# Between the mixtures: the residual as an identity product, row sums and centred squares on ScalarE

## The reference, cut to what matters

```python
def _layernorm(x, axis=-1, eps=1e-05):
    m = jnp.mean(x, axis=axis, keepdims=True)
    v = jnp.var(x, axis=axis, keepdims=True)
    return (x - m) / jnp.sqrt(v + eps)
...
    def _L1_xattn_ref(hidden_states, memory_tokens, memory_mask):
...
        scores = jnp.einsum('bsd,bmd->bsm', hidden_states, memory_tokens) * scale
...
        attn = jax.nn.softmax(scores, axis=-1)
        readout = jnp.einsum('bsm,bmd->bsd', attn, memory_tokens)
...
    x = x + _L1_xattn_ref(_layernorm(x, axis=-1), ctx_2048, mask_BxS2_bk0)
    x = x + _L1_ffn_ref(_layernorm(x, axis=-1), L1_ffn_router_w, L1_ffn_w_gate, L1_ffn_w_up, L1_ffn_w_down)
```

## Time and profile before

| | us |
|---|---|
| median of three timed executions | 1752.46 |
| lowest, highest | 1746.93, 1753.07 |
| the profiled execution | 1746.06 |
| its span, first to last instruction | 1744.3 |
| mean granted TensorE clock (1 is 2.4 GHz, 0.50 is 1.2 GHz) | 0.929 |
| the stage `middle`, SyncE's first load to VectorE's last list | 848.5 to 1001.2 |

### The profile page before, as it was taken

How to read it: one execution, slowest core, us unless ns; L and a number is a source line. 1 busy time by engine, 2 the same in 40 slices (tenths; PEclk the granted TensorE clock), 3 DMA queues, 4 the chain that set the end, 5 groups by cost and what they waited for, 6 DMA issues and landing times. The chain is left out here.

```text
span 1744.3 us, 34265 instructions
## 1 busy us (share of the span) xinstructions
PE 1519.5 (87%) x8762; PEld 1174.2 (67%) x8763; DVE 1364.7 (78%) x2831; ACT 1060.6 (61%) x2044; POOL 777.8 (45%) x515
## 2 busy tenths in 40 slices
PE   4578899998888989999589569999999999999990
PEld 3546666666566867777347348888887778878880
DVE  6835867867787458888377869999999999999992
ACT  1124645635454468887134158888888888888870
POOL 5010000110301325554101248887887878788870
PEclk9588999999999999999775679999999999999995
DMA  9215537354560367755735129888888888998778
GB/s 338 98 44 131 117 74 213 79 119 125 119 184 1 98 228 173 159 107 91 207 116 192 64 73 215 173 174 186 189 186 185 167 209 196 236 215 164 132 121 308
DMA packets 170175, 270.58 MB, mean 155 GB/s; under 512 B 20080, under 2 KB 95856, under 8 KB 167856
## 3 DMA queue, kind: packets, MB, share of 16 engines
q0 software_dynamic: 46448, 108.85, 32.5%
q1 hardware_dynamic: 123632, 160.57, 31.2%
HBM read 151.62 MB, written 91.16 MB: 139 GB/s over the span
## 5 line engine op out<-in xcount | busy, mean ns | idle before, releaser
L1969 DVE TENSOR_TENSOR moe_w_lo<-moe_w_up,moe_w_hi 128x1536 fp32r<-128x1536 f32 (+1 forms) x180 | 325.9, 1811 | 1.7 <-ACT moe_w_hi L1793 1.7
L1744 POOL DMA_INDIRECT moe_rows<-moe_rows,moe_ids x200 | 282.4, 1412 | 66.7 <-issue 58.8
L1793 ACT ACTIVATE moe_w_hi<-moe_w_up 128x1536 fp32r (+2 forms) x180 | 273.7, 1520 | 0.0
L2082 PE MATMUL psum<-moe_w_hi,moe_rows_hi 128*128 128x384 f32 (+1 forms) x720 | 262.8, 365 | 3.6 <-DVE moe_rows_lo L1963 3.6
L2083 PE MATMUL psum<-moe_w_lo,moe_rows_hi 128*128 128x384 f32 (+1 forms) x720 | 248.7, 345 | 0.0
L2084 PE MATMUL psum<-moe_w_hi,moe_rows_lo 128*128 128x384 f32 (+1 forms) x720 | 248.7, 345 | 0.0
L1755 POOL DMA_INDIRECT moe_sum<-moe_res,moe_ids x100 | 189.6, 1896 | 96.4 <-ACT moe_res L1831 48.4
L1755 POOL DMA_INDIRECT moe_other<-moe_res,moe_ids x100 | 187.6, 1876 | 87.6 <-ACT moe_res L1831 38.2
L2092 PE MATMUL psum<-moe_w_down,moe_hid_t 128*128 (+1 forms) x400 | 205.0, 594 | 0.0
L862 ACT ACTIVATE prob<-psum,neg_top 128x128 f32<-128x128 f32 (+3 forms) x256 | 133.1, 528 | 80.2 <-DVE neg_top L1052 74.9
L1963 DVE TENSOR_TENSOR moe_rows_lo<-psum,moe_rows_hi 128x512 fp32r<-128x512 f32 x200 | 138.3, 691 | 19.5 <-ACT moe_rows_hi L1776 12.6
(11 more groups left out here) (356 smaller groups left out, 3367.1 us busy)
## 6 DMA issues: line engine op xcount, KB each, us to landing
q_st<-unit SPq DMA_DIRECT2D x128, 128.0 KB, 3.0
k_st<-unit SPq DMA_DIRECT2D x128, 128.0 KB, 3.1
moe_w_up<-in_L_ffn_w_gate SPq DMA_DIRECT2D x32, 384.0 KB, 5.2
moe_w_up<-in_L_ffn_w_up SPq DMA_DIRECT2D x32, 384.0 KB, 6.1
moe_w_down<-in_L_ffn_w_down SPq DMA_DIRECT2D x32, 256.0 KB, 6.5
moe_w_down<-in_L_ffn_w_down SPq DMA_DIRECT2D x64, 128.0 KB, 7.0
moe_sum<-x_sb SPq DMA_DIRECT2D x4, 1024.0 KB, 4.4
moe_sum<-m_x_sb SPq DMA_DIRECT2D x4, 1024.0 KB, 4.7
```

The lines of the kernel that those rows point to most:

```text
L1744: pool.indirect_dma_start(rows[u][:, :], None, d["rows"], bass.IndirectOffsetOnAxis(ids[:, t:t + 1], 0)).then_inc(gathered[u], 16)
L1793: sc.activation(w_hi[u % SPLITS][:, :], up_of(at), ACT.Copy).then_inc(T["wh"], 1)
L1969: v.tensor_tensor(w_lo[u % SPLITS][:, :], up_of(at), w_hi[u % SPLITS][:, :].bitcast(F32), ALU.subtract).then_inc(T["wl"], 1)
L2082: mm(ps[:, 2 + i, 0:2 * I], hi, w_h, start=(k == 0), stop=False)
```

## The change

It does four things between the mixtures.

1. The residual: after each attention product a second product, of the identity with the tile of x, adds x into the same PSUM bank. VectorE's `residual` is gone; ScalarE copies the bank into x and sums the rows on the way.
2. Statistics: ScalarE makes minus the mean from the row sum, then squares each tile with that as bias and sums the squares. VectorE makes the variance from them (`variances`, `second_variances`). This holds for the second norm of all batches and for the first norm of batches 1 to 3. The row sum of those comes from the addition of the tables. The squares themselves are written to places that are overwritten later.
3. The two filler products between logits and `attended` are gone.
4. Orders: the context is loaded after two pairs of tables; GpSimd's norm of batch 3, VectorE's softmax of batch 0 and sums of batch 3, and ScalarE's rows stand elsewhere.

The core of the diff:

```diff
@@ sync
-            sp.dma_start(ctx_sb[:, :, :], a["ctx_2048"].rearrange("b k d -> k b d")).then_inc(S["ctx"], 16)
             tables(0, 2, x_in[0])
             tables(2, 2, x_in[1])
+            sp.dma_start(ctx_sb[:, :, :], a["ctx_2048"].rearrange("b k d -> k b d")).then_inc(S["ctx"], 16)
...
@@ gpsimd
-            first_norm(3)
             for b in range(BATCH - 1):
                 second_norm(b + 1)
+                if b + 3 < BATCH:
+                    first_norm(b + 3)
                 write_runs(pool, m, b, run_ids[b][:, :], r1["slots"], S["slotted"])
...
@@ scalar
+            def squares(u, b, spare):
+
+                act.wait_ge(S[f"minus{u + 1}"], b + u)
+                for t in range(TPB):
+                    n = tile(b, t)
+                    sc.activation(spare(b, t), x[:, n, :], ACT.Square, bias=minus[u][:, n:n + 1],
+                                  accum_out=square[u][:, n:n + 1]).then_inc(S[f"square{u + 1}"], 1)
+
+            def minus_mean(u, b):
+                of_batch = slice(tile(b, 0), tile(b + 1, 0))
+                sc.activation(minus[u][:, of_batch], total[u][:, of_batch], ACT.Copy, scale=-1.0 / D).then_inc(S[f"minus{u + 1}"], 1)
+
+            def statistics(b):
+                act.wait_ge(S["added"], b)
+                minus_mean(0, b)
+                squares(0, b, lambda b, t: xn[:, t, :])
+
+            def residual(b):
+                for t in range(TPB):
+                    n = tile(b, t)
+                    act.wait_ge(S["o"], n + 1)
+                    sc.activation(x[:, n, :], ps[:, 6 + t % 2, :], ACT.Copy, accum_out=total[1][:, n:n + 1]).then_inc(S["x3"], 1)
+                act.wait_ge(S["x3"], tile(b + 1, 0))
+                minus_mean(1, b)
+                squares(1, b, lambda b, t: hn[:, tile(b, t), :])
...
@@ vector
+                        own.did(v.scalar_tensor_tensor(x[:, n, :], x[:, n, :], 1.0, x_other[:, n, :], ALU.mult, ALU.add,
+                                                       accum_out=total[0][:, n:n + 1]))
...
+            def variances(b):
                 of_batch = slice(tile(b, 0), tile(b + 1, 0))
+                dve.wait_ge(S["square1"], TPB * b)
+                v.tensor_scalar(var[:, of_batch], square[0][:, of_batch], 1.0 / D, EPS, ALU.mult, ALU.add).then_inc(S["var"], 1)
...
-                    v.tensor_tensor(at, at, ps[:, 6 + t % 2, :], ALU.add).then_inc(S["x3"], 1)
...
+            def second_variances(b):
+                dve.wait_ge(S["square2"], TPB * (b + 1))
+                v.tensor_scalar(var2[:, :], square[1][:, tile(b, 0):tile(b + 1, 0)], 1.0 / D, EPS, ALU.mult, ALU.add).then_inc(S["var2"], 1)
...
             add_tables(1)
-            statistics(1)
+            softmax(0)
+            variances(1)
+            shares(0)
             shift_of(1)
-            softmax(0)
-            shares(0)
             add_tables(2)
-            residual(0)
+            second_variances(0)
...
@@ tensor
-                    mm(ps[:, 6 + t % 2, :], att_t[:, t, :], ctx_sb[:, b, :], start=True, stop=True).then_inc(S["o"], 1)
+                    o = ps[:, 6 + t % 2, :]
+                    mm(o, att_t[:, t, :], ctx_sb[:, b, :], start=True, stop=False)
+                    mm(o, ident, x[:, tile(b, t), :], start=False, stop=True).then_inc(S["o"], 1)
...
                 if b + 1 < BATCH:
-                    keep_busy(nc, m, c, 2, 5, True)
                     attended(b + 1)
```

More of the change, by code:

```diff
@@ L2196, in middle @@
         shift, shift2 = sb("shift", [P, TILES]), sb("shift2", [P, TPB])
+        total, minus, square = [[sb(f"{n}{u}", [P, TILES]) for u in range(2)] for n in ("sum_of", "minus", "square")]
         r = {n: sb("r_" + n, [P, TPB, size]) for n, size in (("prob", N), ("logit", N), ("value", 8), ("total", 1), ("mask", N))}
@@ L2310, in _ @@
             normed_out(0)
-            normed(1)
+            statistics(1)
             exponents(0)
             attention_out(0)
+            normed(1)
+            residual(0)
             for b in range(BATCH):
@@ L2317, in _ @@
                     normed_out(b + 1)
+                if b + 2 < BATCH:
+                    statistics(b + 2)
                 hidden(b)
@@ L2327, in _ @@
                     normed(b + 2)
+                if ahead:
+                    residual(b + 1)
         @block.vector
@@ L2362, in shift_of @@
                 dve.wait_ge(S["rstd"], b + 1)
[L2363 removed]
+                v.tensor_tensor(shift[:, of_batch], minus[0][:, of_batch], rstd[:, of_batch], ALU.mult).then_inc(S["shift1"], 1)
             def shift_of_hidden(b):
                 dve.wait_ge(S["rstd2"], b + 1)
[L2367 removed]
+                v.tensor_tensor(shift2[:, :], minus[1][:, tile(b, 0):tile(b + 1, 0)], rstd2[:, :], ALU.mult).then_inc(S["shift2"], 1)
             def softmax(b):
@@ L2384, in shares @@
                 v.tensor_tensor(att[:, :, :], att[:, :, :], den[:, :].unsqueeze(2).to_broadcast([P, TPB, KEYS]), ALU.mult).then_inc(S["p"], 1)
-            def residual(b):
-                for t in range(TPB):
-                    dve.wait_ge(S["o"], tile(b, t) + 1)
-                    at = x[:, tile(b, t), :]
-                    v.tensor_tensor(at, at, ps[:, 6 + t % 2, :], ALU.add).then_inc(S["x3"], 1)
-                    dve.wait_ge(S["x3"], tile(b, t) + 1)
-                    own.did(v.bn_stats(stats2[:, t, :], at))
-                own.wait()
-                for t in range(TPB):
-                    own.did(v.bn_aggr(mv2[:, t, :], stats2[:, t, :]))
-                own.wait()
-                v.tensor_scalar(var2[:, :], mv2[:, :, 1], EPS, None, ALU.add).then_inc(S["var2"], 1)
+            def second_variances(b):
+                dve.wait_ge(S["square2"], TPB * (b + 1))
+                v.tensor_scalar(var2[:, :], square[1][:, tile(b, 0):tile(b + 1, 0)], 1.0 / D, EPS, ALU.mult, ALU.add).then_inc(S["var2"], 1)
             def shift_logits(b):
@@ L2454, in _ @@
             add_tables(0)
-            statistics(0)
+            statistics()
             normed(0)
@@ L2494, in _ @@
                 if ahead:
-                    residual(b + 1)
+                    second_variances(b + 1)
             run_starts(BATCH - 1)
```

33 lines of the change are left out of this document (16 added, 17 removed).

## The result

| | us |
|---|---|
| after, median of four executions | 1796.3 (1783.12 to 1803.01) |
| before, measured beside it, four executions | 1752.76 (1746.93 to 1753.77) |
| ratio | 1.023, 95% interval 1.018 to 1.0281 |
| profiled execution of after | 1783.12, span 1781.3, mean clock 0.913 |

The change makes the kernel 2.3% slower, 43.5 us by the medians. The forecast, 1782, had the direction; the time lies 5 us above the upper end of its range, 1791.

The account below looks back on a forecast made before the run. TensorE at half clock was taken to bound the long stretch, a chain between engines the short ones. Batches +35.8, start -3.5 and end +3.1 gave +35.4 us on 1746.06, 1781.5, taken as 1782; range 1756 to 1791.

Parts of the forecast that it names:

- Direction and mechanism: Stage between the mixtures: ScalarE's copy and squares make TensorE pause, the clock falls after batch 0 and stays down; +35.4 us.
- eight products: Attention plus identity products of one batch on TensorE: 14.25 us at half clock, 7.3 at full.
- third flip: Next batch's third tile flip, waiting for ScalarE to empty a bank: starts 4.55 us after the last product, bounds 4.3 and 5.0.
- logits stage: Part of a batch between scores and transposes: 10.2 us at half clock.
- transposes and copy: Small transposes and their copy ahead of a batch's eight products: 1.75 us at half clock.
- Sum of three: Three batches at half clock, 39.4 us each: 118.2 us where before are 82.4, so +35.8.
- Start: Stage start up to batch 0's last product: reordered loads and earlier softmax end it sooner, -3.5 us.
- End: After the last batch's products: 6.9 us to the first normed flip instead of 4.9, logits at half clock; +3.1 us.
- B: Rival: identity products bring the clock back within each eight; +23.4 us, 1769 us; chance 0.22.
- D: Mixed rival: the clock falls in only one or two of three batches, 12 us each above C; 1756 to 1768; chance 0.13.
- C: Rival: full clock throughout, pairs carrying it over the waits; batch 27.4 us, -2.2 us, 1744 us; chance 0.1.
- Row sums: VectorE's table sums gain a row sum: between nothing and 0.2 us more each, taken as 0.1.

Follow-up runs that it names:

- e8: The changed kernel without identity products: VectorE adds out of PSUM with a row sum, ScalarE still squares the new rows; stage 163.4 us, ratio 1.0212.
- e3: The changed kernel with the residual's part undone, so VectorE adds and takes those statistics again; stage 145.9 us, ratio 0.9914 from five of ten executions.
- e7: The kernel before with only the identity products added, VectorE copying where it added, fillers kept; stage 172.6 us, ratio 1.0199.
- e2: The changed kernel with ScalarE emptying the next batch's four flips before squaring the residual's tiles; stage 189.0 us, ratio 1.0264.
- e13: The changed kernel with four filler products in each of two pauses per batch, behind the second flip and behind the scores; stage 172.5 us, ratio 1.0181.
- e11: The changed kernel with attention products widened from 64 to 128 partitions by zeros; stage 170.5 us, ratio 1.0177.
- second executions: The kernel before and the changed kernel, both unchanged, each profiled once more; stages 147.6 and 188.6 us.
- e14: e13 with the attention products also widened to 128 partitions by zeros; stage 155.6 us, ratio 1.0063.
- e5: The kernel before with only the two filler products ahead of each batch's transposes taken out; stage 144.7 us, ratio 1.0103.
- e1: The changed kernel with the two filler products before each batch's transposes put back; stage 173.1 us, ratio 1.0171.
- e9: e3 with the attention products widened from 64 to 128 partitions by zeros; stage 142.5 us, ratio 1.0049.

## Why the prediction was right and wrong

**Direction and mechanism: right.** After's stage was forecast at +35.4 us against the profiled execution, and that pair of profiles gives +38.2. ScalarE's copy and squares ahead of the emptying, TensorE's pause, the clock at half in the eight products of all batches but the first (with brief rises elsewhere that the forecast did not have), and VectorE idle for over 10 us are all there. e8 and e3 show what ScalarE's work on the new rows costs, e7 what the doubled products cost. That the pause itself brings the clock down is shown as far as this: it falls inside the pause in the change, in e8 and in e2, and with the pauses filled (e13) it stays up. It can fall without such a pause too (e3).

**One batch, term by term** (902.01 to 942.9): third flip 4.71 us after the last product (forecast 4.55); two flips 1.74 (1.8); scores 6.71 (6.9); logits stage 10.1 (10.2); transposes and copy 1.73 (1.75). These hold within 0.2. **The eight products are the mis-sized term, and the step that failed**: 16.0 us for 14.25. I put 1.78 on each, the time between products of one kind; alternating kinds take 2.00, and e11 shows that it is the alternation. That is 1.75 us a batch, 5.25 in three. The last batch is 2.6 us short of the others, because its logits saw the clock up for a while. Sum of three: 120.1 for 118.2.

**Start** -3.6 (forecast -3.5): the last product of batch 0 ended 37.2 us after the first load, where 40.8 had been. The second executions gave 38.5 and 40.9, so -2.4. **End** +4.1 (forecast +3.1): from the last product to the first hidden flip 7.15 us (1022.05 to 1029.20, forecast 6.9), and the rest is the logits at half clock. In the second executions the end gave only +1.6, for the kernel before took 31.5 us there and not 29.1. That all three terms came so near is in part luck of the two executions: the second pair has +41.8 in the batches.

**Why the time left the range.** I took the sum to the profiled execution, 1781.5, and kept 1782, although the text said that from the median it was 1788. The range was to hold the other, but its upper end, 1791, held only 3 us over that sum. The eight products, 5.25 us too cheap, take 1788 to 1793.5 by themselves. As for the 14.8 us from 1781.5 to 1796.3: 6.7 are the base (1752.8 for 1746.1). Another 4.2 are the stage: the mean of two executions each gives +39.6, not +35.4. In the first pair the excess is 2.8, the products' 5.25 and 1 at the end, less 2.6 in the last batch and some 0.7 in the smaller terms. The rest is that 152.3 was a long stage for the kernel before, which had 147.6 in its second execution. The last 3.9 us are within what executions of one program differ by, and I can't name them further.

**The rivals.** B, that identity products bring the clock back, fell: a set that starts at half stays there to its end (e7), and it is the 64-partition half of each pair that holds it down (e11). D is what e13 shows, one set up and two down, but with fillers that the change doesn't have. C's batch at full clock, 27.4 us, was near what e14 measured, 27.5 (7.1 of them products, 7.3 in the case), but in a version with fillers and widened products. Its 1744, no loss, was not reached: the stage of e14 is 155.6 us, and the kernel before without fillers has batches of 24.6 to 25.3 us at a mean clock of only 0.70 (e5). So a change that held the clock up would still not be a gain. The fillers, which I left out at half clock, were worth more than their time ahead of eight products in the profiled execution of e1, which no case had.

**Row sums.** A table sum with row sum, in VectorE's order of the changed kernel:

```profile
881.27 0.69 DVE L2377 SCALAR_TENSOR_TENSOR m_x_sb<-m_x_sb,m_x_other 128x512 f32<-128x512 f32 x1 [0.21 <-DMA m_x_other<-moe_other]
881.88 0.08 DVE L2377 DVE_READ_ACCUMULATOR m_x_sb<-m_x_sb,m_x_other 128x1 f32 x1
881.88 0.69 DVE L2377 SCALAR_TENSOR_TENSOR m_x_sb<-m_x_sb,m_x_other 128x512 f32<-128x512 f32 x1
```

One follows the other after 0.61 us, and the plain add took 1.29 us for two, 0.69 for one and so 0.60 from one to the next. The form costs 0.01 us more at most, and I had taken 0.1. The half throughput that the Trainium skill ("Vector Engine (DVE) Microarchitecture Reference", section "Points that are easy to get wrong") gives for this form with two 32-bit sources in SBUF did not show.

## What to carry to other kernels

Before work moves to an idle engine, look at what that engine does next in its queue and who waits for it: here some 3 us of squares ahead of an emptying cost 4.5 to 6 us a batch (e8 against e3), because behind TensorE's pause the clock was down as well, and the doubled products cost another 9 at that clock. Price a matmul that is added to an accumulator from products in the same alternation, not from a row of like ones, and at both clock levels. And set a sum against more than one profiled execution where the clock comes and goes.

## What the hardware showed that I had not expected

- Products over 64 and 128 partitions in turn take 2.00 us each at half clock and 1.05 at full; all over 128 partitions, 1.70 and 0.86.
- With the same columns, four products over 64 partitions that began at half clock left it down (7.2 us, 0.50 throughout, e3, e5 and e8), and over 128 it came back inside them (5.7 us, e9). Zeros in the other 64 partitions were enough.
- VectorE's two-source operation with a row sum runs at the pace of the plain add, 0.61 us for 512 elements of each row; its sum is read in 0.08 us, and the next one starts at the same time.
- The clock fell in waits of quite different length: 3.54 us in e8, but also behind waits of 0.98 and 1.23 us in e3, while it outlasted one of 1.09 us in e13.
- The code ahead of the stage and behind it, the same in all versions, differs between their executions by up to 21 us ahead and 22 behind; what causes it was not looked into.
